# Two buffers for rounded tokens, a shared norm scratch, and statistics, copies and a gate product in new places

## What is computed

```python
def _layer(x, wqkv, qs, ksc, wo, lg, lb, w1, b1, w2, b2):   # B=8, 512 tokens, 8 heads of 64, window 64
    h = shift_token(x)
    q, k, v = to_heads(split(h @ wqkv))
    q, k = rotary_xpos(l2norm(q) * qs, l2norm(k) * ksc)
    x = x + local_attention(q, k, v) @ wo
    h = shift_token(x)
    h = (h - mean(h)) / sqrt(var(h) + 1e-05) * lg + lb
    a, g = split(h @ w1 + b1)                                # 341 columns each
    return x + (a * gelu(g)) @ w2 + b2

x = x + 0.5 * ffn(_layernorm(x))        # ffn: the two layers, one after the other
x = x + mla(_layernorm(x))              # causal attention with a latent of 64, 16 heads of 8
x = x + 0.5 * ffn(_layernorm(x))
```

## Time and profile before

| | |
|---|---|
| median of 3 runs | 2055.65 us (2052.55 to 2056.91) |
| the profiled execution | 2055.3 us, its span 2053.5 us |
| TensorE busy | 1709.2 us, 83% of the span |
| VectorE, ScalarE, GpSimd busy | 1339.8, 918.1, 798.9 us (65%, 45%, 39%) |
| mean granted TensorE clock | 0.950 |
| first feed-forward phase, from its first row | 31.7 us |

### The profile page before, as it was taken

The page is one execution under the profiler, slowest core; times in us unless marked ns, Lnnn a source line. Parts: engine busy times, 40 slices in busy tenths (PEclk is TensorE's granted clock), DMA queues, the critical chain, the costliest instruction groups (busy, mean ns, idle before and its releaser), DMA issues. The chain is left out here.

```text
span 2053.5 us, 47885 instructions
## 1 busy us (share of the span) xinstructions
PE 1709.2 (83%) x19752; PEld 993.1 (48%) x19818; DVE 1339.8 (65%) x2021; ACT 918.1 (45%) x1455; POOL 798.9 (39%) x561
## 2 busy tenths in 40 slices
PE   3678888898988887799999994788888899888886
PEld 2344455555555554355555542444445555555543
DVE  3577777667776663567777754567777666667752
ACT  2234444445455443145555552344544454445542
POOL 2545444455555451100000003455554554455530
...
DMA packets 82762, 148.55 MB, mean 72 GB/s; under 512 B 15039, under 2 KB 25715, under 8 KB 80371
## 3 DMA queue, kind: packets, MB, share of 16 engines
...
...
## 5 line engine op out<-in xcount | busy, mean ns | idle before, releaser
L951 POOL TENSOR_TENSOR QK<-QK,RB 128x1024 f32<-128x1024 f32 x128 | 303.1, 2369 | 437.6 <-DMA RB<-RN 436.7
L791 DVE SCALAR_TENSOR_TENSOR TP<-banks,cols,tab 128x1024 f32<-128x1024 f32 x256 | 321.0, 1275 | 98.1 <-PE banks L455 82.0
L945 POOL TENSOR_TENSOR QK<-TP 128x512 f32<-128x512 f32 x128 | 164.7, 1287 | 274.1 <-DVE TP L791 215.8
L1288 ACT ACTIVATE PTL<-banks 128x1024 f32<-128x1024 f32 (+1 forms) x192 | 168.3, 884 | 168.4 <-PE banks L1195 168.4
L1363 DVE TENSOR_REDUCE NM<-banks 128x2 f32<-128x1024 f32 (+3 forms) x256 | 203.2, 819 | 57.4 <-PE banks L1164 56.5
L814 DVE TRANSPOSE_TENSOR_REDUCE MX<-banks 128x16 f32<-128x512 f32 x256 | 160.1, 681 | 62.8 <-PE banks L492 62.8
L647 ACT ACTIVATE SQ<-banks 128x512 f32<-128x512 f32 x128 | 76.6, 598 | 277.5 <-PE banks L455 277.5
L832 DVE TENSOR_TENSOR OT<-banks,OT 128x512 f32<-128x512 f32 x128 | 85.3, 687 | 162.1 <-DMA OT<-sums_d 146.8
L455 PE MATMUL banks<-HTH,wqkv_h 128*128 128x512 f32 x256 | 126.6, 495 | 66.4 <-POOL HTL L937 39.3
L946 POOL TENSOR_TENSOR QK<-TP 128x512 f32<-128x512 f32 x128 | 165.4, 1292 | 0.0
L675 ACT ACTIVATE PT<-banks 128x512 f32<-128x512 f32 x256 | 132.2, 602 | 49.3 <-PE banks L506 49.3
...
## 6 DMA issues: line engine op xcount, KB each, us to landing
RB<-RN SPq DMA_DIRECT2D x512, 64.0 KB, 4.0
OT<-sums_d SPq DMA_DIRECT2D x128, 256.0 KB, 4.0
...
RB<-vars_d SPq DMA_DIRECT2D x32, 256.0 KB, 3.3
rows_d<-HIGH SPq DMA_DIRECT2D x32, 256.0 KB, 3.0
QS<-rows_d SPq DMA_DIRECT2D x32, 256.0 KB, 2.7
KS<-rows_d SPq DMA_DIRECT2D x32, 256.0 KB, 3.0
```

Of the source, the lines that this page charges most:

```text
L791: nc.vector.scalar_tensor_tensor(out=TP[:, o:o + 2, :], in0=BK[4 + z][:, :].unsqueeze(1).to_broadcast([P, 2, T]), scalar=q, in1=tab[:, e, ...
L945: nc.gpsimd.tensor_tensor(QK[:, m, 0, :], TP[:, 2, :], TP[:, 1, :], ALU.subtract)
L951: nc.gpsimd.tensor_tensor(QK[:, m, :, :], QK[:, m, :, :], RB[:, m, :].unsqueeze(1).to_broadcast([P, 2, T]), ALU.mult).then_inc(S["nr_ok"], 1)
L1288: nc.scalar.activation(PTL[:, G % 2, h0:h0 + 2, f * T:f * T + WIDTH_T[f]], PAIR[at_t(m) % RING][:, :, 0:WIDTH_T[f]], ACT.Exp).then_inc(S[" ...
```

## The change

HTH gets two buffers, used by the parity of the unit. ACT's wait before rounding is then for the products of two units before, and the wait for the products of the unit before stands with GpSimd at HTL. NT_ is gone: the Newton step uses the first plane of SQ as scratch, and ACT's first square of a unit also waits for the Newton step of the unit before. On VectorE `statistics` goes from behind the second `maxima` to the end of the step and one unit further ahead, and `arrive` goes from behind `attended` 1 and `back` to right behind `clamp`. On TensorE the second gate product goes ahead of `project` 0. In the setup block the small rows have their own semaphore and come first, the bias matmuls stand ahead of the weight chain, and x of batches 2 to 7 is loaded by SP at the start of the first feed-forward phase.

```diff
-                    sp.dma_start(cst[:, :], consts[:, o:o + 2 * P + 33]).then_inc(in_small, 16)
-                    x_load(0)
+                    sp.dma_start(cst[:, :], consts[:, o:o + 2 * P + 33]).then_inc(in_rows, 16)
...
+                    x_load(0)
                     for dst, src in ((uq, W_uq), (wom, W_o), (dq, W_dq), (uv, W_uv), (uk, W_uk), (dkv, W_dkv)):
                         sp.dma_start(dst[:, :], src).then_inc(in_small, 16)
...
-                    for b in range(2, NB):
-                        x_load(b)
                     sp.wait_ge(copied, 8)
...
                 def _(pe):
+                    pe.wait_ge(in_rows, ROWS)
+                    pe.transpose(BK[7][:, 0:14], rows[:, :], ident[0:14, 0:14]).then_inc(mm, 1)
                     pe.wait_ge(in_small, SMALL)
                     pe.transpose(BK[0][0:QL, 0:P], uq[:, :], ident).then_inc(mm, 1)
                     pe.transpose(BK[1][:, 0:P], wom[:, :], ident).then_inc(mm, 1)
-                    pe.transpose(BK[7][:, 0:14], rows[:, :], ident[0:14, 0:14]).then_inc(mm, 1)
-                    pe.wait_ge(copied, 1)
-                    nc.tensor.matmul(BK[3][:, 0:P], uqT[:, :], dq[:, :], start=True, stop=True).then_inc(mm, 1)
...
                     last.then_inc(mm, 1)
+                    pe.wait_ge(copied, 1)
+                    nc.tensor.matmul(BK[3][:, 0:P], uqT[:, :], dq[:, :], start=True, stop=True).then_inc(mm, 1)
...
-                HTH = sb("HTH", [P, T])
+                HTH = sb("HTH", [P, 2, T])
...
-                NT_ = sb("NT_", [P, T])
...
                     def _(sp):
+                        if load:
+                            for b in range(2, NB):
+                                sp.dma_start(X[:, b * NT:(b + 1) * NT, :],
+                                             x[b].rearrange("(t p) c -> p t c", p=P)).then_inc(x_in[b], 16)
                         for last_use in used:
                             sp.sem_clear(last_use)
...
                             run(join, n - 2, 7)
+                            run(hidden, n - 3, 1, 1, 6)
                             run(project, n, 0)
-                            run(hidden, n - 3, 1, 1, 6)
                             run(scores, n - 1, 0)
...
-                            if u >= 1:
-                                act.wait_ge(S["v_in"], 4 * u)
-                                act.wait_ge(S["pr_in"], 4 * u)
-                            nc.scalar.activation(HTH[:, :].bitcast(F32R), Z[:, b, 0:T], ACT.Copy).then_inc(S["hth_ok"], 1)
+                            if u >= 2:
+                                act.wait_ge(S["v_in"], 4 * (u - 1))
+                                act.wait_ge(S["pr_in"], 4 * (u - 1))
+                            nc.scalar.activation(HTH[:, u % 2, :].bitcast(F32R), Z[:, b, 0:T], ACT.Copy).then_inc(S["hth_ok"], 1)
...
                             if u >= 1:
                                 act.wait_ge(S["ss_in"], u)
+                                if m == 0:
+                                    act.wait_ge(S["nw_ok"], u)
...
-                            link(nc.vector.scalar_tensor_tensor(out=NT_[:, :], in0=RN[:, :], scalar=-0.5, in1=RN[:, :],
+                            link(nc.vector.scalar_tensor_tensor(out=SQ[:, 0, 0, :], in0=RN[:, :], scalar=-0.5, in1=RN[:, :],
...
                             run(maxima, n - 1, 1)
-                            run(statistics, n + 1)
                             run(rotate, n, 3, 1)
...
                             run(tokens, n + 1)
                             run(clamp, n, 7)
+                            run(arrive, n + 1, 7)
                             run(attended, n - 1, 0, 6)
                             run(norms, n)
                             run(attended, n - 1, 1, 6)
                             run(back, n - 3, 7)
-                            run(arrive, n + 1, 7)
                             run(attended, n - 1, 2, 4)
                             run(attended, n - 1, 3, 5)
+                            run(statistics, n + 2)
                             run(residual, n - 1, 7)
...
                             pool.wait_ge(S["hth_ok"], u + 1)
-                            nc.gpsimd.tensor_tensor(HTL[:, :].bitcast(F32R), Z[:, u % NB, 0:T], HTH[:, :],
+                            if u >= 1:
+                                pool.wait_ge(S["v_in"], 4 * u)
+                                pool.wait_ge(S["pr_in"], 4 * u)
+                            nc.gpsimd.tensor_tensor(HTL[:, :].bitcast(F32R), Z[:, u % NB, 0:T], HTH[:, u % 2, :],
```

67 lines of the change are left out of this document (35 added, 32 removed).

## The result

| | before | after |
|---|---|---|
| median of the runs, us | 2056.28 (2052.55 to 2059.23, 4 runs) | 2032.01 (2025.67 to 2036.71, 4 runs) |
| ratio after / before | | 0.9881, 95% interval 0.9849 to 0.9913 |
| profiled execution, us (span, granted clock) | 2055.3 (2053.5, 0.950) | 2031.05 (2029.3, 0.946) |

The changed kernel is 1.2% faster, and the forecast of 2035 was 3 us from it. The rest of this text asks whether the terms of the sum were right too. Two of them were not (the statistics and `arrive`), and the worth of the setup stays open.

A forecast was written before the change was run, and what follows sets the result against it. The bound was a loop from `maxima` through VectorE, `clamp`, ACT, SP and DMAs, no engine alone. 2055.3 less 16.0 (loop, two phases) less 4.5 (setup) gave 2034.8, forecast 2035; own range 2031 to 2041, 8 in 10: 2022 to 2050.

The forecast's parts named there:

- Statistics: VectorE, `maxima` to `clamp` in the first layer: moving them out gains 1.39 us in step 1, 1.69 in steps 2 to 6.
- CB's hold: VectorE's CB waits until GpSimd's rstd ends, so CB ends at 296.34 instead of 298.03: gain 1.69 us.
- CB not held: Rival: rstd doesn't hold VectorE's CB, steps 2 to 6 gain 0.49 us more, 4.9 in all: 2030; chance 0.12.
- The new place of the statistics: End of the step on VectorE, in its idle time before `residual` (151.8 us, waiting for `join`): costs nothing.
- `arrive`: VectorE behind `clamp`, waiting for TensorE's transposes: costs 0.9 us in step 0, 0.5 in steps 1 and 2, per phase.
- Cost in steps 3 to 6: nothing: Early `arrive` delays the Newton step, but SP's slack shrinks from 2.05 to 0.5 us and norm rows leave as before.
- HTH in two buffers, gate product, norm scratch: TensorE, ACT and GpSimd edits: each worth nothing; gate product bounded by -0.2 and +0.2 us in about 26 steps.
- The slower rival: At VectorE's wait L778, `arrive` holds the Newton step past SP's cover, 1 us per us in 14 steps: 2070; chance 0.06.
- SP's cover: SP is busy with the sums until 308.95, so a Newton step ending near 308.44 doesn't delay its norm rows.
- The rival by which the second buffer gains up to 39.3 us: The second HTH buffer removes up to all of TensorE's HTL waits, 39.3 us: 1996; chance 0.04.
- Setup: Block before the first phase: store of `fold` goes 3.0 us earlier, then 1.5 more; gain 4.5, bounds 3.0 and 5.3.

The follow-up runs named there:

- e2_stats: The kernel before with only the statistics moved to the end of the step and one unit ahead: 2032.68 us, ratio 0.9893.
- e1: The kernel before with only the setup edits, loads of x moved included: 2052.83 us, ratio 0.9987.
- e4: The kernel before with only HTH in two buffers and the norm scratch in SQ: 2057.35 us, ratio 1.001.
- e5: The kernel before with only the second gate product moved ahead of the first `project`: 2056.19 us, ratio 1.0003.
- e6: The changed kernel with `arrive` back at its old place, behind `attended` 1 and `back`: 2027.27 us, ratio 0.9853.
- v2: The changed kernel with `attended` 0 put ahead of the early `arrive`: 2022.04 us, ratio 0.9828.
- e7_wide: The changed kernel with an added, unused GpSimd power of 128x96 elements ahead of rstd: 2418.68 us in one execution.
- e3: The kernel before with only `arrive` moved to right behind `clamp`: 2068.07 us, ratio 1.0057.
- v4_old_setup: The changed kernel with old `arrive` place and old setup, U moved to the end of the step ahead, statistics and rstd further ahead: 2019.39 us, ratio 0.9817.

## Why the prediction was right, and where it was not

**Statistics: they were the gain, and CB's hold was wrong.** The sum had 19.7 us. e2_stats has 22.0 by its ratio (17 to 27), which allows 19.7 as well as the 24.6 without a hold. The trace is sharper. Steps 3 to 6 average 290.5 in the four kernels with the statistics at the old place and `arrive` late (before, e1, e4, e5) and 275.7 in the four with the new one (after, e2, e6, v2). That is 14.8 less in six steps, where six times 1.69 is 10.1 and six times 2.17 is 13.0. Steps 0 to 3, without the kernels that moved `arrive`, fall from 283.3 to 270.2, 13.1 less, but this column swings with the clock. Both together make 27.9, an upper end. The step that failed is "I take the same for CB: 295.80 + 0.54 = 296.34", the hold through rstd. CB was not held, the stretch shrank by 2.17 and not 1.69, and the rival "CB not held" is what happened (it says 2.18; its rows, 298.03 less 295.86, give 2.17). It was given 0.12. VT's row had been read well: what holds is over when that operation ends. The mistake was to take any GpSimd operation as one that holds. e7_wide shows that the power doesn't, even at 15.64 us. With 2.18 in steps 2 to 6 the sum would have had those 24.6.

The rule of the Trainium skill (SBUF — State Buffer, section "Who interferes with whom") would have CB blocked until rstd ends. The traces don't agree for this operation: 0.68 us for CB inside rstd, 0.68 inside 15.64 us of power. For the subtraction HNL they do agree: CB 1.46 us before, held till it ended. Here the measurement decides: a GpSimd power isn't a holder, a GpSimd product or difference is.

**The new place of the statistics costs nothing: right.** VectorE's wait for `join` fell from 151.8 us to 123.6 in the changed kernel. It is still there behind the statistics:

```profile
303.01 0.68 DVE L845 TENSOR_TENSOR Z<-banks,Z 64x512 f32<-64x512 f32 x1 [2.14 <-PE banks L541]
```

**`arrive`: step 5 came out as written, the cost did not.** In step 5 the Newton step at 4.98 (forecast 5.0) and the norm rows at 5.56 came out as written, and TensorE's remaining idle time was 0.37 (forecast 0.8). In six other steps the norm rows were later than 5.6, through SP's own list. "Cost in steps 3 to 6: nothing" holds within the changed kernel: 274.7 us, against 276.1 on average in e2, e6 and v2. On top of the kernel before the table doesn't tell: e3 has 293.3, but e5, with `arrive` late, has 292.9. For steps 0 to 2 the sum had 3.8 us in both phases. Alone, on the old loop, `arrive` cost 11.7 us (7.4 to 16.0), and there the term was clearly too small. In the changed kernel it is 5.8 by the runs of e6, which with its intervals allows 3.8 and nothing as well. The column 0 to 3 would give 7.9 (278.1 against 270.2, the average of e2 and e6), clock included.

Two things were left out of the term. The first is `attend` 1, idle 20.6 us in 12 times for `attended` 0, one for each of steps 1 to 6 in both phases. I had only asked whether idle time behind it covers that. With the swap of v2_attended this wait is gone, and that kernel is 10 us faster than the changed one. That is more than taking `arrive` back gains (e6), by 5 us, with intervals that overlap. How much of the 10 us is this wait, the earlier Newton step or the clock stays open. The second is that the Newton step now stands behind TensorE's queue, so a stretch at the low clock ahead of the transposes goes into it. The changed kernel has that in step 2 of the first phase (sums of squares 3.64 us at a granted clock of 0.50, `attend` 1.51, the transposes ended 2.3 behind `clamp`, the norm rows left at 6.49) and in steps 1 and 2 of the second (6.47 and 6.57). With the same stretch and a late `arrive`, step 2 of e2_stats has its norm rows at 6.10, so the early one adds 0.4 to 0.5 there.

**The slower rival** named the right place (VectorE's wait ahead of the copies) and a price of 1 us for each us past the cover. In e3_arrive the Newton step was past SP's cover in some steps, not in 14, by less than 1 us where the norm rows followed it. On the old loop this edit alone made the kernel slower, by 11.7 us. Under the statistics' gain no such cost could be seen in the total.

**HTH in two buffers, gate product, norm scratch: nothing, right.** 1.001 (0.9996 to 1.0024) and 1.0003 (0.9986 to 1.0019). The reason given for HTL, GpSimd's order, shows in e4_hth. The rival by which the second buffer gains up to 39.3 us is out.

**Setup: the trace exceeds the forecast, the runs are below it.** The last eviction ended at 22.33 (forecast 23.4), and the next block began 3.56 us behind the store (forecast 3.76). So it began 5.8 us earlier, above my bounds of 3.0 to 5.3. The part that was off is the chain of weights: its first product started at 14.85 before and at 18.57 now, 3.7 us later and not the 4.77 that I added. The transposes ahead of it start 0.7 sooner (13.04, before 13.76), and the 0.46 us that TensorE waited for their eviction lies behind the bias matmuls now. In the total the setup has 2.7 to 3.4 us in e1_setup and 4.5 in v4_old_setup. Why 6 us at the first `clamp` should give less in the end isn't settled. The intervals of both allow 6 us.

**The sum.** The errors cancelled, as far as the runs tell: the statistics' gain was about 2 us too small (by the table up to 8), `arrive`'s cost about 2 too small, and the setup's gain 0 to 2 too large. None of these is clear of the noise of the runs in the changed kernel. That the forecast came within 3 us is partly luck. What was forecast well is which part carries the time.
